# Attention of a two-layer mixture-of-experts kernel: head pairs overlapped one pair deeper, with the turned row sums in another bank

## What is computed

```
x = x + s * g                      # layer 0: recurrent mixer s, 8 experts g
xn = _layernorm(x)
q, k, v = proj(wq, bq), proj(wk, bk), proj(wv, bv)      # 16 heads of 64
attn = softmax((q @ k.T) * scale)                       # 256 x 256 for each head
ctx = attn @ v
s = ctx @ wo.T + bo
g = _silu(_L1_ffn_ref(xn, ...))    # 160 experts, 8 for each token
x = x + s * g
```

## Time and profile before

| | us |
|---|---|
| median of 3 runs | 1999.31 (1998.68 to 2007.2) |
| the profiled execution | 1999.14, of which the span 1997.3 |
| first half of attention, first to last score matmul | 853.5 to 1276.3 |
| experts, first to last turn of slots | 1282.0 to 1507.2 |
| second half of attention, first to last score matmul | 1547.1 to 1983.5 |
| share of the span that PE, DVE, ACT and POOL are busy | 88%, 60%, 49%, 34% |
| mean granted clock of PE | 0.948 of full |

### The profile page before, as it was taken

How to read it: one execution, slowest core, us unless ns; L and a number is a source line. 1 busy time by engine, 2 the same in 40 slices (tenths; PEclk the granted TensorE clock), 3 DMA queues, 4 the chain that set the end, 5 groups by cost and what they waited for, 6 DMA issues and landing times.

```text
span 1997.3 us, 47676 instructions
## 1 busy us (share of the span) xinstructions
PE 1750.2 (88%) x13222; PEld 1445.1 (72%) x13309; DVE 1208.2 (60%) x4593; ACT 971.0 (49%) x3034; POOL 687.6 (34%) x735
## 2 busy tenths in 40 slices
PE   5889999999999996787888888899997888777878
PEld 2557699999999776465666666699995666565656
DVE  4553445555555677866666766666663666666667
ACT  2311244444444224365666666655552666555656
POOL 0034412222222004255555555300003555555552
PEclk9988999999999998798999999999998899999999
DMA  9901101111110302111111111377672111111111
GB/s 355 373 21 34 35 24 37 37 37 37 37 37 26 87 0 99 78 34 42 65 39 66 41 64 39 111 197 197 197 198 74 36 45 38 41 42 42 44 42 30
DMA packets 153598, 153.77 MB, mean 77 GB/s; under 512 B 17027, under 2 KB 132294, under 8 KB 153286
## 3 DMA queue, kind: packets, MB, share of 16 engines
q1 hardware_dynamic: 130404, 104.23, 16.5%
q0 software_dynamic: 22272, 47.29, 7.8%
q10 hardware_dynamic: 866, 1.58, 0.2%
HBM read 71.10 MB, written 81.94 MB: 77 GB/s over the span
## 4 chain that ended last, share of the span: by engine, by line
PE 60%; DVE 14%; another core or an unknown queue 9%; issue 8%; ACT 7%; DVEq 1%; DMA 1%; ACTq 0%
PE ps_y L861 7%; ACT probs L741 5%; PE ps_up L1045 4%; PE ps_y L919 4%; PE ps_up L910 4%; PE ps_up L1140 4%; PE ps_t L1157 4%; PE ps_y L1058 3%; PE ps_rec L874 3%; PE ps_rec L876 3%; PE ps_t L879 3%; PE ps_t L877 3%; PE ps_rec L1015 3%; DVE xn_buf L1734 3%
## 5 line engine op out<-in xcount | busy, mean ns | idle before, releaser
L567 POOL DMA_INDIRECT rows_g<-ys_dram,slot x256 | 248.7, 971 | 446.7 <-DMA ys_dram<-slots_y 241.7
L741 ACT ACTIVATE probs<-ps_up,xn_buf 128x256 f32<-128x256 f32 x512 | 236.4, 477 | 191.0 <-DVE xn_buf L1734 166.1
L555 POOL DMA_INDIRECT xs_dram<-xn_buf,slot x256 | 247.3, 966 | 198.3 <-issue 89.8
L1734 DVE TENSOR_REDUCE xn_buf<-ps_up 128x2 f32<-128x512 f32 x256 | 166.9, 687 | 208.9 <-remote 123.6
L1058 PE MATMUL ps_y<-misc,probs 128*128 128x128 f32 x1024 | 171.6, 298 | 115.6 <-ACT probs L741 92.2
L1058 PEld LDWEIGHTS ps_y<-misc,probs 128*128 128x128 f32 x1024 | 117.2, 148 | 161.6 <-ACT probs L741 135.0
L861 PE MATMUL ps_y<-zeros 128*128 128x512 bf16 x660 | 193.8, 388 | 1.8 <-issue 0.2
L1354 DVE SCALAR_TENSOR_TENSOR mixn<-ps_rec,cols_sb,th_r 128x16 f32<-128x16 f32 x256 | 59.8, 233 | 217.7 <-ACT th_r L625 116.9
L525 POOL DMA_INDIRECT ys_dram<-slots_y,row_ids x80 | 78.1, 977 | 300.9 <-DVE slots_y L1484 240.3
L718 ACT COPY probsT<-ps_y 128x512 f32<-128x512 f32 x256 | 147.8, 598 | 32.9 <-remote 16.4
L1078 PE MATMUL ps_t<-probsT,v_sb 128*64 128x256 f32 x1024 | 143.1, 400 | 5.9 <-ACT probsT L718 3.3
(11 more groups left out here) (250 smaller groups left out, 4364.6 us busy)
## 6 DMA issues: line engine op xcount, KB each, us to landing
xn_buf<-xs_dram SPq DMA_DIRECT2D x88, 256.0 KB, 2.8
xs_dram<-zeros SPq DMA_DIRECT2D x42, 512.0 KB, 5.7
ys_dram<-slots_y SPq DMA_DIRECT2D x84, 256.0 KB, 2.4
slots_x<-xs_dram SPq DMA_DIRECT2D x41, 130.0 KB
xs_dram<-zeros SPq DMA_DIRECT2D x10, 520.0 KB, 4.6
gate<-w_gate SPq DMA_DIRECT2D x1, 5120.0 KB, 15.9
down<-w_down SPq DMA_DIRECT2D x8, 640.0 KB
w_sb<-w POOLq DMA_DIRECT2D x16, 256.0 KB, 3.0
```

The source lines that it names most:

```text
L555: nc.gpsimd.indirect_dma_start(xs_dram, bass.IndirectOffsetOnAxis(ap=slot[:, n, k:k + 1], axis=0), xn_tok[:, n, :], None).then_inc(scatter ...
L567: nc.gpsimd.indirect_dma_start(rows_g[:, i % 16, :], None, ys_dram, bass.IndirectOffsetOnAxis(ap=slot[:, i // TOPK1, i % TOPK1:i % TOPK1 + ...
L741: nc.scalar.activation(probs[:, a, i, :], ps_s[a][:, T * i:T * i + T], ACT.Exp, bias=negmax[:, a, i:i + 1], accum_out=sums[:, j % 4, i, a: ...
L1734: V.tensor_reduce(negmax[:, a, :], ps_s[a][:, :].rearrange("p (i t) -> p i t", i=2), AX_X, ALU.max, negate=True).then_inc(max_ready, 1)
```

## The change

Three steps of the chain move one turn later with respect to the scores, and the order on PE is new. In turn p, PE now runs scores of p, `turn_probs` of p-1, `v_mm_` of p, `turn_rsums` of p-2, `values` of p-2, `project` of p-3, `qk_mm` of p+2. ACT copies the turned probabilities of p-1 after the exponentials of p. DVE normalises p-3, takes out the values of p-1, and inverts and spreads the row sums of p-1. The turned row sums go to the right half of the values' bank (`ps_v`) rather than that of the contexts' bank. POOL's waits on `tr_done` are shifted by two, and each half gets a longer tail. The number of matmuls, copies and DMAs is the same. The diff, cut to its core:

```diff
@@ POOL: scatters, then gathers
                     if n and k % 2 == 0:
-                        pool.wait_ge(tr_done, (n * TOPK1 + k) // 2 - 3)
+                        pool.wait_ge(tr_done, (n * TOPK1 + k) // 2 - 1)
...
-                        pool.wait_ge(tr_done, 2 * HB * PAIRS + (i - 16) // 2)
+                        pool.wait_ge(tr_done, 2 * HB * PAIRS - 2 + (i - 16) // 2)
@@ ACT
-                nc.scalar.copy(rsumsT[:, :], ps_ctx[:, T:2 * T]).then_inc(rsumsT_ready, 1)
+                nc.scalar.copy(rsumsT[:, :], ps_v[:, T:2 * T]).then_inc(rsumsT_ready, 1)
...
                     exps(p, j, 1, not early)
+                    if not (first and j < 2):
+                        rsums_out(p - 2, not (first and j == 2))
                     if not early:
-                        rsums_out(p - 1, not (first and j == 1))
-                    probs_out(p, 0, not early)
-                    probs_out(p, 1, not early)
+                        for a in range(2):
+                            probs_out(p - 1, a, not (first and j == 1))
@@ PE
-                    last = nc.tensor.transpose(ps_ctx[:, T + P * i:T + P * i + P],
+                    last = nc.tensor.transpose(ps_v[:, T + P * i:T + P * i + P],
...
                     both_scores(j)
+                    if not early:
+                        for a in range(2):
+                            turn_probs(p * 2 - 2 + a, p - 1, a, not (first and j == 1))
+                    v_mm_(b, j, p, x)
                     if not (first and j < 2):
-                        project(p - 2, (j - 2) % PAIRS, None if first else b)
-                    v_mm_(b + (j + 1) // PAIRS, (j + 1) % PAIRS, p + 1, x)
-                    if not early:
-                        values(p - 1, (j - 1) % PAIRS, not (first and j == 1))
-                        turn_rsums(p - 1)
-                    for a in range(2):
-                        turn_probs(p * 2 + a, p, a, not early)
+                        turn_rsums(p - 2)
+                        values(p - 2, (j - 2) % PAIRS, not (first and j == 2))
+                    if not (first and j < 3):
+                        project(p - 3, (j - 3) % PAIRS, None if first else b)
                     qk_mm(b + (j + 2) // PAIRS, (j + 2) % PAIRS, p + 2, x)
...
                 p = (b0 + HB) * PAIRS
-                project(p - 2, PAIRS - 2, None)
+                for a in range(2):
+                    turn_probs(2 * p - 2 + a, p - 1, a, True)
+                pe.wait_ge(v_ready, p)
+                turn_rsums(p - 2)
+                values(p - 2, PAIRS - 2, True)
+                project(p - 3, PAIRS - 3, None)
+                pe.wait_ge(normed, p - 1)
+                turn_rsums(p - 1)
@@ DVE
-                    if not (first and j < 2):
-                        normalise(p - 2)
-                    values_out(p, j, x, not (first and j < 2))
-                    if j == 2 and not first:
+                    if not (first and j < 3):
+                        normalise(p - 3, not (first and j == 3))
+                    if not early:
+                        values_out(p - 1, (j - 1) % PAIRS, not (first and j < 3))
+                    if j == 3 and not first:
                         output_out(b - 1)
...
-                    invert_sums(p, j)
+                    if not early:
+                        invert_sums(p - 1, j + 3, not (first and j == 1))
                     side_work(b, j, x, (2, 3))
-                    spread_sums(p, not early)
+                    if not early:
+                        spread_sums(p - 1, not (first and j == 1))
```

More of the change, by code:

```diff
@@ L753, in attend @@
                     exps(p, j, 1, not early)
+                    if not (first and j < 2):
+                        rsums_out(p - 2, not (first and j == 2))
                     if not early:
-                        rsums_out(p - 1, not (first and j == 1))
-                    probs_out(p, 0, not early)
-                    probs_out(p, 1, not early)
-                    if j == PAIRS - 2:
+                        for a in range(2):
+                            probs_out(p - 1, a, not (first and j == 1))
+                    if j == PAIRS - 1:
                         copy_inputs(b + 1, x)
@@ L780, in attend_half @@
                     attend(b, x, False)
-                rsums_out((b0 + HB) * PAIRS - 1, True)
+                p = (b0 + HB) * PAIRS
+                rsums_out(p - 2, True)
+                for a in range(2):
+                    probs_out(p - 1, a, True)
+                rsums_out(p - 1, True)
                 if x == 0:
@@ L1182, in attend_half @@
                 qk_mm(b0, 0, b0 * PAIRS, x)
-                v_mm_(b0, 0, b0 * PAIRS, x)
                 qk_mm(b0, 1, b0 * PAIRS + 1, x)
@@ L1193, in attend_half @@
                 values(p - 1, PAIRS - 1, True)
-                turn_rsums(p - 1)
+                project(p - 2, PAIRS - 2, None)
                 if x == 0:
@@ L1679, in qk_low, with values_out @@
                 last.then_inc(qk_ready, 1)
-            def values_out(p, j, x, waits):
-                dve.wait_ge(v_mm, p + 1 + x)
+            def values_out(p, j, waits):
+                dve.wait_ge(v_mm, p + 1)
                 if waits:
@@ L1687, in values_out, with invert_sums @@
                     .then_inc(v_ready, 1)
-            def invert_sums(p, j):
+            def invert_sums(p, j, waits):
+                if waits:
+                    dve.wait_ge(recip_done, p)
                 dve.wait_ge(exp_done, p * 4 + 4)
@@ L1700, in spread_sums, with normalise @@
                               inverse[:, :].unsqueeze(2).to_broadcast([P, 4, HD])).then_inc(recip_done, 1)
-            def normalise(p):
+            def normalise(p, waits):
                 dve.wait_ge(pv_done, p + 1)
                 dve.wait_ge(rsumsT_ready, p + 1)
+                if waits:
+                    dve.wait_ge(out_done, p)
                 V.tensor_tensor(ctxT[:, :], ps_ctx[:, 0:T], rsumsT[:, :], ALU.mult).then_inc(normed, 1)
@@ L1762, in attend_half @@
                 p = (b0 + HB) * PAIRS
+                normalise(p - 3, True)
+                values_out(p - 1, PAIRS - 1, True)
+                invert_sums(p - 1, PAIRS - 1, True)
+                spread_sums(p - 1, True)
                 for k in (2, 1):
-                    normalise(p - k)
+                    normalise(p - k, True)
                 output_out(b0 + HB - 1)
```

## The result

The changed kernel takes **2051.6 us** (median of 4, 2048.54 to 2068.55) against 2000.26 for the kernel before on the same chip (median of 4): ratio 1.027, 95% interval 1.021 to 1.033. It is slower by 51 us where 78 us of gain were forecast, outside the range.

What follows compares the result with a forecast made beforehand. Attention was taken as bound by PE waiting behind late signals, each turn about 5.1 + L. First half -36, second -41, tails +4, clock -5: -78 from 1999.1, so 1921 us; range 1872 to 1985.

Steps and rivals of the forecast that it cites:

- PE's floor: Attention turn, score matmul to score matmul with no pause on PE: 5.1 us, unchanged because all matmuls stay.
- the chain of 4.0 + L: New attention turn: scores, maxima, low part of keys, queries and keys; the turn is the larger of 5.1 and this.
- L: Distance from the recorded end of the scores on PE to the start of DVE's maxima; mean taken as 1.7 us.
- The 0.65 us a turn: Net saving per attention turn: mean 0.67 us over three turns shown, lowered for the move's additions on DVE.
- Rival (a): Attention signals held while PE has no pause: turn 7.2 us, 2054 us in all, from mean L above 2.8; 11%.
- The exponentials' new wait at 0: ACT's first exponential of p waits for the turn of p-1, which ends early enough on PE: cost 0.
- ACT's copies "just in time", at 0: ACT's copies of p-1 behind the exponentials of p, at 0.65 us, reach PE in time: cost 0, little to spare.
- POOL's waits as an edit without a price: Second half: gathers 1.25 us apart, 5.0 us a pair, under PE's floor, so no bound; that half gives 41 us.
- The clock: Attention, PE's granted clock: pauses up to 1.1 us shorter, a sixth of the slow stretches gone, -5 us.
- POOL's cap of 36 us: First half: scatters need 5.98 us a pair, last one ends at 1237 rather than 1272.8, so at most 36 us.
- Tails, +4: Behind each half's last scores, contexts and projection of one more pair with a normalisation: some 2 us, twice.
- The rule weighed: Increments queue at about 26 ns: no signal over 0.1 us late, turn 5.1, second half gives 115 us; 1850 us, 2%.

Runs made afterwards that it cites:

- a_gather_0: The changed kernel with only the gathers' wait on `tr_done` put back from -2 to +0, late session: 1981.5 us, ratio 0.991 to the kernel before.
- a_nodma2: The changed kernel without the scatters and all but the first 16 gathers, late session: 1767.5 us, ratio 0.884 to the kernel before.
- a_oldpool: The changed kernel with POOL's two waits on `tr_done` as they were before, quiet session: ratio 0.995 to the kernel before.
- after_again: The changed kernel, unchanged, run again beside the kernel before in a late session: 2055.9 us, ratio 1.028.
- a_nodma: The changed kernel without the scatters and all but the first 16 gathers, quiet session: 1770.3 us, ratio 0.961 to the kernel before.
- b_nodma: The kernel before without the scatters and all but the first 16 gathers, quiet session: 1784.6 us, ratio 0.969 to the kernel before.
- b_gather_p2: The kernel before with the gathers' wait on `tr_done` at +2, late session: 1988.1 us, ratio 0.995 to the kernel before.

## Why the prediction was wrong

- *PE's floor and the chain of 4.0 + L.* Right in the turn shown: 5.97 us at L = 1.95; without late signals the turn is at PE's floor, 5.0 rather than 5.1.
- *L unchanged at its mean of 1.7.* This step failed. The 1.7 was all of a turn above 5.1; read turn by turn, mean L was 1.30 and 1.55 us. The forecast took each turn's L from before and let the new order run past it. It grew by 0.78 us in the first half and, at the old gathers' wait, by 0.70 in the second, against savings of 0.98 and 1.07 behind the exponentials. The 0.65 us a turn came out as 0.05 and 0.3. Rival (a) had named a longer L ("signals may be held while PE has no pause") and set its point at a mean L of 2.8; the means are 2.08 and 1.54, so its 2054 us is met by luck. Counted over turns with two indirect DMAs started in the 3 us ahead of the scores' end, L is 1.6 us before, 2.5 in the first half of the changed kernel and 2.3 in a_gather_0 (in the changed kernel's second half, with its long pauses, 1.5): as many DMAs, other order of PE. That a pause of PE lets signals out is not shown. The long turn speaks against it: the signal for the second head's exponentials came 2.5 us after PE had stopped (1688.93 to 1691.47).
- *The exponentials' new wait at 0.* Failed, above all in the second half: 0.43 + 0.44 us a turn in the table of means, 55 us over 63 turns. There it is nearly 0 (0.05 us) with the old gathers' wait. The prediction looked at how early the turns end, not at how late their signal comes, though it had L in hand for the scores.
- *ACT's copies "just in time", at 0.* PE's turns wait for them 42.6 us, 26 times, in the changed kernel. These waits come with late signals too, as at 1696.11.
- *POOL's waits as an edit without a price.* The largest failure. The prediction checked that gathers could keep up (1.25 us apart, "no bound") and stopped there. In the new order the -2 unties the gathers from PE. That is worth 74 us, and the sign. The way it acts is argued, not shown: DVE's four rows no longer wait for the exponentials of their turn between the second and the third, so nothing spaces the gathers.
- *The clock.* 5 us of gain forecast; the mean fell from 0.948 to 0.930, and is 0.953 at the old gathers' wait. In the long turn above the matmuls run at half pace behind a pause of 3.62 us, as in the earlier trace rows.
- *POOL's cap of 36 us.* Its last scatter was to come at 1237; with late signals it came at 1275.7, in a quiet session at 1232.1, where the first one had started 20 us earlier (811.8 against 832.0). The bound exists, but the 5.98 us was 0.6 us a pair too small, so the first half could have given some 20 us and not 36, by an estimate from 832.0 + 420.3.
- *Tails, +4.* 3.3 us in the second half; in the first hidden behind the last scatter.
- *The rule weighed.* The rule of the Trainium skill, "TensorE: Matmul & The Clock Gate", section "The cost: per-tile semaphore tail", has increments on matmuls queue at about 26 ns each and leaves no room for an L of 2 us; the late sessions speak against it. Without the indirect DMAs, or in a quiet session, nothing does: L is 0.03 in the median of the first half (a_nodma2, a_oldpool).

## What to carry to other kernels

A wait that only paces an engine is part of the schedule: when an order is changed, cost its loosening like any other edit, and try each value apart from the order, for here the order was worth -1% and the pace that came with it +3.7%. Where a signal is known to be late, every new wait on that engine's signals has that lateness for its price, and a chain that is shortened may be refilled by it. And run the kernel before beside every experiment: 8 to 9% lay between sessions here, and the late signals were absent from three of five.

## What the runs showed of the hardware

- Indirect DMAs started by POOL can hold back PE's semaphore increments. From the records of after_again's second half, by the number of such DMAs started in the 3 us before a matmul ended, the mean delay of its increment was 0.02 us (none), 0.08 (one), 2.6 (two) and 4.4 (three); without the DMAs (a_nodma2, same session) none is over 0.05 in either half. Some per cent of the increments are missing from the trace, and the means are over those that could be matched.
- It depends on something outside the program. In three of the five sessions (same 0.95 us for each indirect DMA on POOL, same 2.05 us from its start to the first of its increments in the median of the scatters) hardly an increment was late, also in runs of over thirty gathers: in a_oldpool's second half the mean delay is 0.02 us with two or three of them. What differs between the sessions is open, and the changed kernel itself was only timed in late ones.
- The records of DMA increments tell the two kinds of session apart, which nothing else here does. Of the 4096 increments of the 256 scatters the traces hold 1633 to 1762 in late sessions (nine traces) and 3900 to 3948 in quiet ones (eight). It is so even where no signal of PE is late: of the 256 of the first 16 gathers, a_nodma2 has 80, a_nodma and b_nodma all. Whether the missing ones are lost in the recording alone, and whether the recording has a part in the lateness, no run here can say.
- Left open besides: whether the run of eight gathers is by itself what the -2 does (the counts of runs and the timeline point to it, the five runs of eight in b_gather_p2 do not; the run that would show it fell in quiet sessions), and whether a second buffer for the probabilities cures the exponentials' wait.
